# Turning x, context and h by DMA instead of on TensorE, with xT on a ring of three entries

## The reference

```
q  = ln(x);  kv = ln(ctx)
qp = q @ Wq.T + bq;  kp = kv @ Wk.T + bk;  vp = kv @ Wv.T + bv
scores = qh @ kh.T / sqrt(32) - scale[h] * |q_xy - tok_xy| + offset[h]
attn = softmax(scores);  x = x + (attn @ vh) @ Wo.T + bo
h = gelu(ln(x) @ W1.T + b1);  x = x + h @ W2.T + b2
```

## Time and profile before

| what | value |
|---|---|
| time of the kernel, median of three | 1340.43 us |
| the profiled execution's own time | 1340.12 us |
| its span, first to last instruction | 1338.3 us |
| what lies around the span | 1.8 us |
| TensorE matmul busy | 1265.7 us, 95% |
| VectorE, ScalarE, GpSimd busy | 888.0, 831.9, 752.0 us |
| mean busy share of the 16 DMA engines, SyncE's queue | 67.7% |
| mean granted TensorE clock | 0.962 |

### The profile page before, as it was taken

The page is one execution under the profiler, slowest core; times in us unless marked ns, Lnnn a source line. Parts: engine busy times, 40 slices in busy tenths (PEclk is TensorE's granted clock), DMA queues, the critical chain, the costliest instruction groups (busy, mean ns, idle before and its releaser), DMA issues.

```text
span 1338.3 us, 29112 instructions
## 1 busy us (share of the span) xinstructions
PE 1265.7 (95%) x10624; PEld 881.7 (66%) x10624; DVE 888.0 (66%) x2299; ACT 831.9 (62%) x1905; POOL 752.0 (56%) x871
## 2 busy tenths in 40 slices
PE   5777668999999999999999999999999999999998
PEld 5556336666767676766667676767677676766664
DVE  6577777857667586867677675868676775656311
ACT  4566667766666666666666666666667676664231
POOL 2244556765756576665647565766656575647310
PEclk9775789999999999999999999999999999999999
DMA  6336769676867776775858676777868686657334
GB/s 232 101 76 157 194 166 216 139 186 143 201 150 185 148 179 157 177 173 150 189 146 202 142 174 162 171 173 161 181 146 194 147 188 135 164 144 182 89 109 142
DMA packets 366830, 216.58 MB, mean 162 GB/s; under 512 B 282192, under 2 KB 307040, under 8 KB 366688
## 3 DMA queue, kind: packets, MB, share of 16 engines
q1 hardware_dynamic: 366688, 214.73, 67.7%
HBM read 109.66 MB, written 12.58 MB: 91 GB/s over the span
## 4 chain that ended last, share of the span: by engine, by line
PE 85%; DMA 4%; ACT 4%; DVE 3%; SPq 2%; issue 1%; POOL 0%; DVEq 0%; ACTq 0%
PE ps_down L585 24%; PE ps_up L571 24%; PE ps_qk L500 11%; PE ps_vo L523 6%; PE ps_vo L526 6%; PE ps_s L537 4%; PE ps_pv L552 4%; DMA c_stage<-in_w 3%; PE ps_pv L558 2%; PE ps_pv L479 2%; ACT square_half L648 1%; SPq L333 1%; PE ps_vo L486 1%; SPq L342 1%; PE ps_up L450 1%
## 5 line engine op out<-in xcount | busy, mean ns | idle before, releaser
L984 DVE CUSTOM_DVE_ANT_0 soft<-ps_s,soft,factor 128x256 f32<-128x256 f32 x512 | 226.6, 480 | 266.5 <-PE ps_s L537 265.4
L571 PE MATMUL ps_up<-hT,w 128*128 128x256 f16 x3072 | 378.5, 273 | 0.0
L585 PE MATMUL ps_down<-w,hid 128*128 128x512 f16 x1536 | 372.6, 379 | 0.6 <-DMA w<-x_scratch 0.3
L571 PEld LDWEIGHTS ps_up<-hT,w 128*128 128x128 f16 x3072 | 301.1, 98 | 87.8
L1156 POOL TENSOR_SCALAR p_nat<-soft 128x512 f16<-128x512 f32 x256 | 182.4, 712 | 268.4 <-ACT soft L704 250.7
L704 ACT ACTIVATE soft<-soft,neg_max 128x256 f32<-128x256 f32 x512 | 255.3, 501 | 106.1 <-DVE neg_max L984 100.7
L736 ACT ACTIVATE u<-ps_up,bias,up_scale 128x256 f32<-128x256 f32 x256 | 143.4, 560 | 172.7 <-PE ps_up L571 171.4
L1163 POOL TENSOR_SCALAR soft<-dist,scale_neg,offset 128x512 f32<-128x512 f32 x256 | 237.9, 929 | 3.3 <-DVE p_nat L995 3.3
L585 PEld LDWEIGHTS ps_down<-w,hid 128*128 128x128 f16 x1536 | 148.3, 97 | 133.7 <-DMA w<-x_scratch 2.4
L995 DVE SCALAR_TENSOR_TENSOR p_nat<-soft,p_nat 128x512 f16<-128x512 f32 x256 | 200.2, 782 | 0.5 <-POOL p_nat L1156 0.5
L697 ACT ACTIVATE qk_parts<-ps_qk,bias_qkv 128x512 f16<-128x512 f32 x128 | 87.7, 685 | 86.8 <-DMA stack<-stack 43.4
(11 more groups left out here) (119 smaller groups left out, 1586.7 us busy)
## 6 DMA issues: line engine op xcount, KB each, us to landing
w<-x_scratch SPq DMA_DIRECT2D x256, 256.0 KB, 2.8
stack<-qk_parts SPq DMA_DIRECT2D x256, 96.0 KB
raw<-in_ctx SPq DMA_DIRECT2D x32, 256.0 KB, 3.4
raw<-in_x SPq DMA_DIRECT2D x32, 256.0 KB, 3.3
c_stage<-in_w SPq DMA_DIRECT2D x8, 1024.0 KB, 6.6
x<-in_x SPq DMA_DIRECT2D x32, 256.0 KB, 4.2
out<-x SPq DMA_DIRECT2D x32, 256.0 KB, 3.3
tok_rows<-in_tok_xy SPq DMA_DIRECT2D x16, 256.0 KB, 4.0
```

What stands on the lines that cost most here:

```text
L571: mm = e.matmul(ps_up[s % 2][:, 0:L], w_1_sb[:, wp, k, m * P:(m + 1) * P], hT[:, b % 2, xp, k, :], start=(k, wp, xp) == (0, 0, 0), stop=(k ...
L585: mm = e.matmul(ps_down[tt][:], hid[:, chunk % HID_RING, i, hp, tt * P:(tt + 1) * P], w_2_sb[:, s % W2_RING, wp, :], start=(m == 0 and (hp ...
L984: e.tensor_tensor_reduce(soft[:, ring, lc, :], ps_s[:, lc * T:(lc + 1) * T], soft[:, ring, lc, :], factor[:, 0:1], 3.0e38, ALU.add, ALU.mi ...
```

## The change

The tiles of x, ctx and h are split before they are turned. ScalarE and VectorE write the HI and LO parts side by side into `x_nat` (one tile) or `h_nat` (one tile for each tt), from SBUF instead of from PSUM. SyncE then issues one DMA transpose of 128 x 1024 float16 for each of the 96 tiles, of the form of `p_turn`. TensorE's 384 transposes are gone. `xT` becomes a ring of three entries, each the two tiles of ctx or of x of one batch; `hT` stays at two batches. To make room `soft` goes from five entries to four and `bias_tile(i)` moves from slot i - 2 to slot i - 1. `stack_copies` move to the head of SyncE's slot, before `p_turn`; the new turns stand behind `p_turn` and before `load_w2`. `norm_apply` of n = 2, 3 moves from slots 0 and 4 to 4 and 7, `h_apply` from the head of slots 11 and 13 to the end of slots 10 and 12. The ring of turned P keeps its six entries. Cut to its core, the diff is:

```diff
-        SOFT_RING, NAT_RING, PT_RING, STACK_RING, DIST_RING, X1_RING, U_RING, HID_RING, W2_RING = 5, 4, 6, 2, 2, 6, 3, 2, 3
-        CH = 4
+        SOFT_RING, NAT_RING, PT_RING, STACK_RING, DIST_RING, X1_RING, U_RING, HID_RING, W2_RING = 4, 4, 6, 2, 2, 6, 3, 2, 3
+        CH, XT_RING = 4, 3
-        xT = sb("xT", [P, 2, 2, 2, KT, L], F16)
+        x_nat = sb("x_nat", [P, 2, D], F16)
+        xT = sb("xT", [P, XT_RING, 2, 2 * KT, P], F16)
-        hT = sb("hT", [P, 2, 2, KT, L], F16)
+        h_nat = sb("h_nat", [P, 2, 2, D], F16)
+        hT = sb("hT", [P, 2, 2, 2 * KT, P], F16)
-        X_TURN, V_PROJ, O_PROJ, H_TURN = -23, (1, 4), (24, 26), (28, 30)
+        X_APPLY, V_PROJ, O_PROJ, H_APPLY = (-24, -20, -12, -9), (1, 4), (24, 26), (26, 28)
+        def xT_of(b, which):
+            return xT[:, (2 * b + which) % XT_RING, :, :, :]
...
@@ sync_program @@
+            def x_turn(b, n):
+                gate.wait_ge(s_xlo, n_tile(b, n))
+                if n < 2:
+                    gate.wait_ge(s_qk, n_qk(4 * (b - 2) + 3, 1))
+                else:
+                    gate.wait_ge(s_qk, n_qk(4 * (b - 1) + 3, 0))
+                    gate.wait_ge(s_v, n_half(b - 1, 1))
+                e.dma_start_transpose(xT_of(b, n // 2)[:, n % 2, :, :], x_nat[:].rearrange("p w d -> p (w d)")).then_inc(s_xt, DMA)
+            def h_turn(b, tt):
+                gate.wait_ge(s_hlo, n_half(b, tt))
+                gate.wait_ge(s_m1, MT * (b - 1))
+                e.dma_start_transpose(hT[:, b % 2, tt, :, :], h_nat[:, tt, :, :].rearrange("p w d -> p (w d)")).then_inc(s_ht[tt], DMA)
...
+                for G in due(slot, QK_PROJ + 4, GROUP, N_HG):
+                    stack_copies(G)
                 for i in due(slot, 3, ITEM, N_ITEMS):
                     p_turn(i)
+                for n in range(4):
+                    for b in due(slot, X_APPLY[n] + 2, BATCH, B):
+                        x_turn(b, n)
+                for tt in range(LC):
+                    for b in due(slot, H_APPLY[tt] + 2, BATCH, B):
+                        h_turn(b, tt)
                 for s in due(slot, DOWN - 2, ITEM, N_STEPS):
                     load_w2(s)
-                for G in due(slot, QK_PROJ + 4, GROUP, N_HG):
-                    stack_copies(G)
...
@@ tensor_program @@
-            def x_turn(b, n):
...
-                for k in range(KT):
-                    tr = e.transpose(ps_pv[:, k * P:(k + 1) * P], raw[:, n, k * P:(k + 1) * P], ident[:])
-                tr.then_inc(s_xtr)
-            def h_turn(b, tt):
...
                     for which, sec in ((0, SEC_K), (1, SEC_Q)):
-                        gate.wait_ge(s_xlo, n_tile(b, 2 * which + 1))
+                        gate.wait_ge(s_xt, DMA * n_tile(b, 2 * which + 1))
...
@@ scalar_program @@
             def x_hi(b, n):
-                gate.wait_ge(s_xtr, n_tile(b, n))
-                gate.wait_ge(s_qk, n_qk(4 * (b - 2) + 3, n // 2))
-                gate.wait_ge(s_v, n_half(b - 2, 1))
-                e.activation(xT_parts(b, n)[HI], turned(ps_pv), ACT.Copy).then_inc(s_xhi)
+                gate.wait_ge(s_ap, n_tile(b, n))
+                gate.wait_ge(s_xt, DMA * (n_tile(b, n) - 1))
+                e.activation(x_nat[:, HI, :], raw[:, n, :], ACT.Copy).then_inc(s_xhi)
             def h_hi(b, tt):
...
+                gate.wait_ge(s_hap, n_half(b, tt))
+                gate.wait_ge(s_ht[tt], DMA * b)
+                e.activation(h_nat[:, tt, HI, :], x1_n[:], ACT.Copy).then_inc(s_hhi)
...
-                    for b in due(slot, X_TURN + 1 + 4 * n, BATCH, B):
+                    for b in due(slot, X_APPLY[n] + 1, BATCH, B):
                         x_hi(b, n)
...
@@ vector_program @@
-                e.tensor_tensor(lo, turned(ps_pv), hi, ALU.subtract).then_inc(s_xlo)
+                e.tensor_tensor(x_nat[:, LO, :], raw[:, n, :], x_nat[:, HI, :], ALU.subtract).then_inc(s_xlo)
-                e.tensor_tensor(lo, turned(ps_vo), hi, ALU.subtract).then_inc(s_hlo)
+                e.tensor_tensor(h_nat[:, tt, LO, :], x1_n[:], h_nat[:, tt, HI, :], ALU.subtract).then_inc(s_hlo)
-                    for b in due(slot, H_TURN[tt] - 1, BATCH, B):
-                        h_apply(b, tt)
...
-                    for b in due(slot, X_TURN + 2 + 4 * n, BATCH, B):
+                    for b in due(slot, X_APPLY[n] + 1, BATCH, B):
                         x_lo(b, n)
...
+                    for b in due(slot, H_APPLY[tt], BATCH, B):
+                        h_apply(b, tt)
...
@@ gpsimd_program @@
-                for i in due(slot, -2, ITEM, N_ITEMS):
+                for i in due(slot, -1, ITEM, N_ITEMS):
                     bias_tile(i)
```

More of the change, by code:

```diff
@@ L248, in build_block @@
             for tt in range(2):
-                vo_uses += [("h", b, tt) for b in due(slot, H_TURN[tt], BATCH, B)]
                 vo_uses += [("v", b, tt) for b in due(slot, V_PROJ[tt], BATCH, B)]
@@ L500, in qk_project @@
                                 mm = e.matmul(ps_qk[:, which * L:(which + 1) * L], w_sec[sec][:, wp, k, hg * P:(hg + 1) * P],
-                                              xT[:, b % 2, which, xp, k, :], start=(k, wp, xp) == (0, 0, 0), stop=last)
+                                              xT_of(b, which)[:, :, xp * KT + k, :], start=(k, wp, xp) == (0, 0, 0), stop=last)
                                 if last:
@@ L509, in vo_project @@
                     kind, b, tt = use
-                    if kind == "h":
-                        continue
                     if kind == "v":
-                        gate.wait_ge(s_xlo, n_tile(b, tt))
+                        gate.wait_ge(s_xt, DMA * n_tile(b, tt))
                         gate.wait_ge(s_wlo, AT[SEC_V] + 1)
@@ L522, in vo_project @@
                             if kind == "v":
-                                mm = e.matmul(ps_vo[:], xT[:, b % 2, 0, xp, k, tt * P:(tt + 1) * P],
+                                mm = e.matmul(ps_vo[:], xT_of(b, 0)[:, tt, xp * KT + k, :],
                                               w_sec[SEC_V][:, wp, k, :], start=first, stop=last)
@@ L563, in mlp_up @@
                 b, m = divmod(s, MT)
-                gate.wait_ge(s_hlo, n_half(b, 1))
+                for tt in range(LC):
+                    gate.wait_ge(s_ht[tt], DMA * (b + 1))
                 gate.wait_ge(s_wlo, n_piece(N_CHUNKS - 1, KT - 1))
@@ L570, in mlp_up @@
                     for wp, xp in PASSES:
-                        mm = e.matmul(ps_up[s % 2][:, 0:L], w_1_sb[:, wp, k, m * P:(m + 1) * P], hT[:, b % 2, xp, k, :],
+                        mm = e.matmul(ps_up[s % 2][:, 0:L], w_1_sb[:, wp, k, m * P:(m + 1) * P], hT[:, b % 2, :, xp * KT + k, :],
                                       start=(k, wp, xp) == (0, 0, 0), stop=(k, wp, xp) == (KT - 1,) + PASSES[-1])
@@ L615, in tensor_program @@
                     vo_ready -= 1
-                for n in range(4):
-                    for b in due(slot, X_TURN + 4 * n, BATCH, B):
-                        x_turn(b, n)
-                for tt in range(LC):
-                    for b in due(slot, H_TURN[tt], BATCH, B):
-                        h_turn(b, tt)
                 for G in due(slot, 8, GROUP, N_HG):
@@ L750, in scalar_program @@
                 for n in range(4):
-                    for b in due(slot, X_TURN + 1 + 4 * n, BATCH, B):
+                    for b in due(slot, X_APPLY[n] + 1, BATCH, B):
                         x_hi(b, n)
                 for tt in range(LC):
-                    for b in due(slot, H_TURN[tt] + 1, BATCH, B):
+                    for b in due(slot, H_APPLY[tt] + 1, BATCH, B):
                         h_hi(b, tt)
@@ L1085, in vector_program @@
                 for n in range(4):
-                    for b in due(slot, X_TURN - 1 + 4 * n, BATCH, B):
+                    for b in due(slot, X_APPLY[n], BATCH, B):
                         norm_apply(b, n)
```

37 lines of the change are left out of this document (8 added, 29 removed).

## The result

The changed kernel takes **1388.09 us** (median of four executions, 1385.36 to 1388.67) against 1340.43: a ratio of 1.035, 95% interval 1.033 to 1.037. The forecast was 1324 us with a range of 1304 to 1346, and a chance of 0.21 on slower. The profiled execution took 1387.5 us, 1385.7 of span, 47.4 more span than before. TensorE's busy time fell from 1265.7 to 1236.9 us, by 29 us and not by the forecast 60; the difference wasn't followed up.

What follows compares the result with a forecast made beforehand. TensorE was taken to bound the steady stretch. From 1340.1 us, -34.8 for the turns, +21.6 for new waits and -2.9 in the preparation gave -16.1, so 1324 us, range 1304 to 1346.

Steps and rivals of the forecast that it cites:

- -34.8 us for the turns: TensorE, steady stretch: removing 79 turns at 0.44 us each gains 34.8 us if nothing else ends later.
- `stack_copies` hide: SyncE, slot 9: copies placed before p_turn cost nothing, since p_turn waits there for attend anyway.
- The lag: x_hi(b, 0) waits for the previous batch's last turn in x_nat, so score_max starts 1.3 us later (0.6 to 5.9).
- Whether TensorE feels it: Slots 10 to 14: VectorE's delay reaches the next scores past 1.48 us of slack; 1.8 us lost a batch (0.5 to 6.5).
- `x_lo` and `h_lo` at +0.1 us each, of which 0.3: VectorE's busy stretch: two SBUF inputs slow four LO parts by 0.1 us each, of which 0.3 a batch counted.
- The late bias tile at 0.35 us: GpSimd, slots 10 and 12: bias_tile one slot nearer stands behind h_rstd; this or a semaphore step costs about 0.35 us a batch.
- +21.6 us for the new waits: Steady stretch: 1.8 us lost in each of 12 batches, b = 4 to 15, sum 21.6 us (6 to 40).
- The preparation, -2.9 with bounds of -11 and +6: First about 240 us: start +4.7, chunk loads -7.6, turns -3, DMA +3, together -2.9 us.
- The gain of the copies first: Preparation: six chunk loads issue sooner with the copies ahead of the wait for attend, -7.6 us.
- DMA at 0.79: 16 DMA engines: 96 transposes raise mean share from near 0.70 to about 0.79, not full; as the bound, a rival at 0.05.
- The rule that would have given 1410: Trainium skill's VectorE page: eight DMA-transposed blocks one after another take an estimated 10.5 us a tile, giving 1410 us.
- The third rival: Slower: the turn of (b-1, 3) lands late, at 5.5 us loss 3.9 a batch, 1349 us; chance 0.17.

Runs made afterwards that it cites:

- e5: Kernel before the change, with the four transposes of every turn made twice (768 instead of 384): 1391.8 us, ratio 1.037 to 1.041.
- e8: e7 with h and the x tile n = 1 one slot later, out of VectorE's slot 13: 1310.6 us, ratio 0.975 to 0.979 to the kernel before.
- e2: Changed kernel with stack_copies moved back behind load_w2: 1363.0 us, ratio 1.016 to 1.021 to the kernel before.
- e1: Changed kernel with tile n = 0 split into the idle second entry of h_nat instead of x_nat: 1337.2 us, ratio 0.996 to 0.9995 to the kernel before.
- e9: e1 with x_lo and h_lo reading one SBUF tensor, subtraction left out, so output is not the reference's: 1327.6 us.
- e7: Changed kernel without x_nat: all x turns in h_nat, n = 1 a slot later, five soft entries, bias_tile back in slot i - 2: 1329.4 us.
- e11: e7 with only bias_tile moved to slot i - 1, as in the change: 1336.1 us, ratio 0.995 to 0.998 to the kernel before.
- e6: Kernel before the change with only stack_copies moved to the head of SyncE's slot: 1335.1 us, ratio 0.995 to 0.997.
- e14: Changed kernel with h and the x tile n = 1 one slot later, nothing else: 1380.0 us, ratio 1.028 to 1.032 to the kernel before.
- e12: Changed kernel with only the h work one slot later (H_APPLY 27, 29 for 26, 28): 1383.2 us, ratio 1.030 to 1.034 to the kernel before.

## Why the prediction was wrong

- **-34.8 us for the turns: right.** e5, the second halves and the period of e8 all show 0.44 us each.
- **"`stack_copies` hide": wrong, the first step that failed.** The copies wait for `qk_lo`, start only 1.67 us before `attend` ends and take 3.26. I had set their length against no start time. In the kernel before `qk_lo` ended 2.7 us before `attend`, already too late by 0.6 for copies of 3.3 us, and the `x_lo` that the change put ahead of it made it 1.0 more. The lag was 2.9 us instead of 1.3. Landing and issue were as forecast (3.2 and 1.3 us). e2 and e1 show the step and its whole.
- **Whether TensorE feels it: a waiter was missed.** I followed the lag only to `score_max`, at 1.8 us a batch where 4.1 or more were lost. Behind it stands `add_residual`, and the second output projection waits for that: 1.7 us a batch in the mean (18.8 us in 11 batches beside the one of 8.4). e1 removes this wait. The wait that I did forecast, of 1 to 2 us in slot 14, came at 2.3, but that is luck: it is still 1.84 in e1, where the lag that I derived it from is gone.
- **`x_lo` and `h_lo` at +0.1 us each, of which 0.3: mis-sized.** It was +0.3 and +0.4 in the mean and +1.07 and +0.41 in slot 13, where both stand in the stretch; e9 got 9.6 us back for a part of it. The mean of `p_lo` was the wrong row, because it says nothing of what GpSimd does beside the new instruction. The timeline of the kernel before had it: `p_lo` took 0.68 us in one place and 1.04 beside GpSimd in another. The Trainium skill (GPSIMD Engine Reference, section Specifications, the row on SBUF interfaces) says that GpSimd contends with VectorE instructions with two SBUF inputs or in a mode that uses two ports. For two inputs the rows agree (1.09 and 1.75 us against 0.64 with GpSimd idle); e9's instruction with one input is stretched too, 809 ns against 381, and no row tells its mode. I had the page in hand and let the mean of another instruction overrule it.
- **The late bias tile at 0.35 us: mis-sized.** Alone it is 1.5 us a batch in the kernel before and 1.6 in the best version (37.25 against 35.66), up to 23 us in all; beside the full slot 13 (e7 to e11) it is under 0.1.
- **+21.6 us for the new waits:** TensorE's waits from 250 us on came to 56.7. They come from the late copies, the missed waiter, the LO parts and the bias tile. The last two hide each other, so the 56.7 can't be shared out among the four.
- **The clock wasn't in the sum:** about 9 us, which follow from the waits. From 260 us on e1 and e8 have none of it.
- **The preparation, -2.9 with bounds of -11 and +6: wrong in sign.** +16.4, of which e1 takes 15.7 away: ScalarE waited for turns there as well (24 us in five waits before 250 us), and I had costed the collision only for b = 4 to 15, and 1.3 us in two slots. Q's projection came 6.2 us later (43.26 us in the chain against 37.09); I had 4.7. The gain of the copies first exists, 6.2 us in e6 against 7.6.
- **DMA at 0.79: 0.82, and not the bound, as said.** A turn took more of the 16 engines than the 1.17 us that I read from two windows: by the shares of the two periods, (0.82 x 76.2 - 0.70 x 74.0) / 6 = 1.8 us. The rule that would have given 1410 (10.5 us a tile) is refuted: half of the tiles land within 3.2 us. It pointed to the right side by the wrong cause.
- **The third rival, at 0.17, has the right sign and place.** It asked for late landings; the turn was issued late instead.

## What to carry to other kernels

Before an operation goes ahead of another in an in-order queue, set its start (what it waits for) beside the end of the wait that should hide it; its length alone says nothing. A staging tile that is shared by producer and DMA chains queues across engines: give each turn that can overlap another its own, or use one that is idle then; here that was 51 us. When two small delays feed one busy stretch, remove both before judging either: moving the slots was worth 2 us or 19, and the early bias tile 7 or 23, depending on the other.

## What the runs showed of the hardware

One VectorE instruction of one shape, two SBUF inputs to float16 128x512, takes 0.64 us with GpSimd idle, 1.09 beside `bias_tile` or `p_hi`, and 1.75 beside GpSimd's 2.23 us addition of `x` and `b`. In the steady stretch of the changed kernel TensorE's granted clock went to the 1.2 GHz level for 3.4 us after four waits of 2.2 to 2.3 us, and stayed at 2.4 GHz after others of 2.27; in e2 it fell after seven of eleven waits of 2.28 to 2.30, in e14 after waits of 2.4 and 2.5, and in e12 once after a wait of 1.89 and after eleven others of 1.89 not. From 260 us on e1, e7 and e8 have no wait over 1.84 us, and there it never fell. What decides in the batches with the same wait wasn't tested.
